# Sorted runs of 16 records instead of 8 in a four-layer graph network kernel

## The chip, the core and the metric

The kernel runs on one core of a Trainium2 chip. The metric is the device time of one execution in microseconds (us). The kernel before the change took 11441.29 us in the median of three runs (11425.31 to 11446.05).

## What is computed

Four graph layers over 12,500 nodes with 64 features and 212,500 directed edges (`src`, `dst`), sorted by `dst`. Each layer takes a layer norm and a relu of `x` and adds its result to `x`. Cut to the steps that matter here:

```python
h = relu(layernorm(x)); x = x + L0(h, edge_attr, src, dst)   # per-feature softmax over the edges of a dst
h = relu(layernorm(x)); x = x + L1(h, src, dst)              # mean of x[src] over the edges of a dst
h = relu(layernorm(x)); x = x + L2(h, src, dst)              # hyperbolic attention, summed by row = src
h = relu(layernorm(x)); x = x + L3(h, src, dst, edge_type)   # relational attention over the edges of a dst

# L2, the part that needs the edges in another order
u, v = -hh[row], hh[col]                  # row = src, col = dst
e = distance(u, v)                        # one number for each edge
attention = softmax of e over the edges with the same row
out[row] = sum of attention * log_h[col]
```

Layers 0, 1 and 3 sum over the edges of one `dst`, and the edges come sorted by `dst`. Layer 2 sums over the edges of one `src`, so the kernel sorts the edges by `src` itself, and only as far as it needs: into 98 blocks of 128 nodes.

## The kernel before

The program is a row of blocks, each with its own instruction streams for the engines, and a block ends when all its streams have ended: a preparation (to about 300 us), `softmax_edges(0)`, `finish_softmax`, `mean_edges`, `finish_mean`, `hyperbolic_edges`, `finish_hyperbolic`, `softmax_edges(3)`, `finish_relational`. The `*_edges` blocks are loops over edges in software-pipelined stages (`steps`, or `unrolled` in the mean loop): each engine runs its stage of several chunks in turn and waits on counters of the others. Four buffer slots (`SLOTS`) let the gathers run ahead.

The sort is spread over the first blocks. Partition p holds 1664 consecutive edges, cut into eight parts g of 208. A record is one float that packs `dst` and the node's place in its block of 128; an empty place holds 0.

- `softmax_edges(0)` counts the edges by block on the side.
- `finish_softmax` (L1512 to L1564) lays out where each group (part g, block b) goes. It pads every group to a multiple of `RUN` records, so that whole runs of `RUN` records can be moved. For each of the `PARTS * NK` pieces of 128 runs one DVE instruction (L1560) works out the runs' destinations, `dest`. POOL meanwhile issues 100 row gathers (L1339), and DVE waits for these afterwards (L1566).
- `mean_edges` sorts one part after another beside its own loop of 208 steps. POOL issues eight row gathers in each step (L922). PE turns the gathered rows (L934), DVE scans them (L1016), and in a turn of the sort DVE builds `hot_high` (L1047), 9 or 10 one-hot rows of `SORTED` columns, ACT builds `hot_low` (L986, L991), and PE multiplies both into `ps_sort` (L953), `SORTED` columns wide.
- `finish_mean` gathers 100 tiles of the mean (L1339), and behind them on the same POOL queue it scatters the sorted runs to `perm` in DRAM (`scatter_runs`, L1332): `PARTS * NK` indirect DMAs of 128 runs each. DVE computes the table of layer 2, and SP stores it with two DMAs (L1727, L1728). POOL waits at its end for the scatters, SP for the stores.
- `hyperbolic_edges` reads `perm` back as `NT` tiles of 128 records and runs `NT / 8` chunks (`CHB`) of eight tiles. A tile belongs to one block of `src`. For each tile POOL gathers 128 rows of `table2` by `dst` (L1148), SP loads the 128 rows of its block (L1134), DVE compares, PE turns the one-hot tile (L1179, moved by ACT at L1212), expands (L1188) and adds up (L1170), DVE carries the sum (L1321), and ACT stores it (L1224).

`NT` is fixed when the program is built, at the most that any graph could need: every group padded by `RUN - 1` and every block's last tile nearly empty, rounded up to 32 tiles. Tiles behind the last filled one are hollow: all their 128 records are 0, so that all 128 gathers of the tile read row 0 of `table2`; they go through the loop like the others.

```python
NK = -(-(P * PC + BLOCKS * (RUN - 1)) // (P * RUN))
SORTED = NK * RUN
NT = SLOTS * BT * -(-(E + PARTS * BLOCKS * (RUN - 1) + BLOCKS * (P - RUN)) // (P * SLOTS * BT))
```

Of the kernel before, what the change touches and what calls it, by code (L numbers as in the profile page):

```python
# [21 lines left out]
ALU = mybir.AluOpType  # L22
# [5 lines left out]
P = 128  # L28
# [17 lines left out]
ACC2 = D + 1  # L46
BLOCKS = -(-N // P)
BT = 8
RUN = 8
PARTS = 8  # L50
PC = PER // PARTS
NK = -(-(P * PC + BLOCKS * (RUN - 1)) // (P * RUN))
SORTED = NK * RUN
NT = SLOTS * BT * -(-(E + PARTS * BLOCKS * (RUN - 1) + BLOCKS * (P - RUN)) // (P * SLOTS * BT))
TRASH = NT * P // RUN
RUNS = TRASH + PARTS * NK * P
# [16 lines left out]
def build(nc, x, src, dst, edge_attr, edge_type, w0a, b0a, gamma, beta, w0b, b0b, scale0,  # L73
          w1, b1, w2, c2, w3, al3, ar3, b3, out):
    with ExitStack() as whole:
        def dram(name, shape, dt):
            return nc.dram_tensor(name, shape, dt, kind="Internal").ap()
# [3 lines left out]
        src3 = dram("src3", (EP,), I32)  # L81
        perm = dram("perm", (RUNS, RUN), F32)
        block_g = dram("block_g", (NT,), I32)
# [18 lines left out]
        def sb(name, shape, dt, ctx=whole):  # L102
            return ctx.enter_context(nc.sbuf_tensor(name, shape, dt))
# [56 lines left out]
        def stepper(eng, sem):  # L160

            count = [0]

            def step(ins):
                count[0] += 1
                ins.then_inc(sem, 1)
                eng.wait_ge(sem, count[0])
            return step
# [645 lines left out]
        def mean_edges():  # L814

            with nc.cleanup_on_exit(), ExitStack() as ctx:
                def buf(name, shape, dt=F32):
                    return sb(f"m_{name}", shape, dt, ctx)
# [18 lines left out]
                slot_i = buf("slot_i", [P, PC], I32)  # L837
                low_i = buf("low_i", [P, PC], I32)
                high_i = buf("high_i", [P, 2, PC], I32)
# [41 lines left out]
                with nc.Block() as block:  # L881
# [118 lines left out]
                    def _(dve):  # L1000
                        v = nc.vector
# [18 lines left out]
                        def divide(g):  # L1020

                            count = [0]

                            def step(ins):
                                count[0] += 1
                                ins.then_inc(split, 1)
                                dve.wait_ge(split, g * 5 + count[0])
                            dve.wait_ge(ranked, g * PC + PC)
                            step(v.tensor_copy(slot_i[:, :], slot_f[:, g, :]))
                            step(v.tensor_scalar(low_i[:, :], slot_i[:, :], 3, P - 1, ALU.logical_shift_right, ALU.bitwise_and))  # L1030
                            step(v.tensor_scalar(minus_low[:, g, :], low_i[:, :], -1.0, None, ALU.mult))
                            v.tensor_scalar(high_i[:, 0, :], slot_i[:, :], 10, 3, ALU.logical_shift_right, ALU.logical_shift_left)
                            step(v.tensor_scalar(high_i[:, 1, :], slot_i[:, :], RUN - 1, None, ALU.bitwise_and))
                            step(v.tensor_tensor(high_f[:, g, :], high_i[:, 0, :], high_i[:, 1, :], ALU.add))

                        def sort(p, w):
                            g = p - 1
                            if w == 0:
                                if g >= 0:
                                    divide(g)  # L1040
                                if p < PARTS:
                                    v.tensor_copy(ps_base[:, 0:BLOCKS], base[:, p, :]).then_inc(based, 1)
                                    dve.wait_ge(based, p + 1)
                            if g >= 0:
                                buffer_free(dve, g, w)
                                n0, n1 = cum(w), cum(w + 1)
                                v.tensor_tensor(hot_high[:, w % 2, 0:n1 - n0, :], ps_columns[:, None, 0:SORTED].broadcast_to([P, n1 - n0, SORTED]),  # L1047
                                                high_f[:, g, n0:n1][:, :, None].broadcast_to([P, n1 - n0, SORTED]),
                                                ALU.is_equal).then_inc(marked, 1)
                            if p < PARTS:  # L1050
                                for n in of_turn(w):
                                    at = p * PC + n
                                    if at >= 4:
                                        dve.wait_ge(ranked, at - 3)
                                    v.scalar_tensor_tensor(junk[:, at % 4, 0:BLOCKS + n], cat[:, p, 0:BLOCKS + n], cat[:, p, BLOCKS + n:BLOCKS + n + 1],  # L1055
                                                           ps_base[:, 0:BLOCKS + n], ALU.is_equal, ALU.mult,
                                                           accum_out=slot_f[:, p, n:n + 1]).then_inc(ranked, 1)
# [351 lines left out]
        def finish_softmax():  # L1409

            with nc.cleanup_on_exit(), ExitStack() as ctx:
# [26 lines left out]
                padded_i = sb("padded_i", [P, 2, HOT], I32, ctx)  # L1438
# [25 lines left out]
                with nc.Block() as block:  # L1464
# [34 lines left out]
                    def _(dve):  # L1499
                        v = nc.vector  # L1500
                        step = stepper(dve, ran)
# [5 lines left out]
                        def flat_b(a):  # L1507
                            return a[:, :, :].rearrange("p (t j) b -> p t (j b)", t=2)
# [1 line left out]
                        last = BLOCKS - 1  # L1510
                        dve.wait_ge(prefixed, 1)
                        step(v.tensor_scalar(padded_i[:, :, :], ps_y[:, :, 0:HOT], float(RUN - 1), None, ALU.add))  # L1512
                        step(v.tensor_scalar(padded_i[:, :, :], padded_i[:, :, :], 3, 3, ALU.logical_shift_right, ALU.logical_shift_left))
                        step(v.tensor_copy(flat_b(padded), padded_i[:, :, :]))
                        row = padded[:, :, :].rearrange("p g b -> p (g b)")
                        step(v.tensor_tensor_scan(out=upto[:, :, :].rearrange("p g b -> p (g b)"), data0=row, data1=row, initial=0.0,
# [508 lines left out]
```

## Time and profile before

| | |
|---|---|
| median of three runs | 11441.29 us |
| the profiled execution | 11452.29 us |
| its span, first to last instruction | 11450.6 us |
| its mean granted TensorE clock | 0.607 |
| PE, DVE, ACT, POOL busy | 59%, 62%, 35%, 67% |

The stages of the profiled execution by the timeline, in us from the span's start: `finish_softmax` 2453 to 2930, the mean loop to 5044, `finish_mean` 5058 to 5632, the hyperbolic loop 5653 to 8388. "Busy" is the time in which an engine carries out an instruction; waits, branches and issuing of a DMA by SP or ACT aren't counted. Idle time is put down to what ended it; "issue" means that the engine waited for nothing the profile shows. The DMA share is that of 16 DMA engines.

### The profile page before, as it was taken

What the parts mean: (1) busy time and instruction counts of PE and PEld (TensorE: products, weight loads), DVE (VectorE), ACT (ScalarE), POOL (GpSimd) and SP (SyncE); (2) the same over time, 40 slices, a digit from 0 to 9 for tenths busy, and PEclk for the clock granted to TensorE, in tenths of its full rate; (3) what the DMA queues carried; (4) which work ended last, traced back from release to release, by engine and by line L of the source; (5) the groups of instructions that cost most, each with busy time, mean ns of one, the idle gap of its engine ahead of it and who ended that gap; (6) DMA issues with size and microseconds to landing.
All of it is one profiled execution on the core that took longest, in us unless ns stands there. A gap on an engine that the chain in (4) does not pass through costs nothing. (4 is left out here: it accounts for less than half of the span.)

```text
span 11450.6 us, 134539 instructions
## 1 busy us (share of the span) xinstructions
PE 6752.2 (59%) x28079; PEld 5273.3 (46%) x28079; DVE 7082.5 (62%) x14431; ACT 4031.5 (35%) x8105; POOL 7668.6 (67%) x7662
## 2 busy tenths in 40 slices
PE   0777777733156666533277777777616677677660
PEld 0444444422045555533177777777613344444440
DVE  3666666663466666624466666666524588888882
ACT  0222222211057666731155555555410133333330
POOL 5777777761577777778666666666542577777774
PEclk9655566555578888865555555555555565555655
DMA  2444444440433333320344444444722344444441
GB/s 79 122 129 129 129 129 129 129 76 7 149 66 67 67 67 66 67 47 8 57 93 91 92 91 92 92 91 91 74 29 70 104 130 128 128 130 127 130 123 40
DMA packets 1419449, 1048.80 MB, mean 92 GB/s; under 512 B 921421, under 2 KB 1138032, under 8 KB 1418781
## 3 DMA queue, kind: packets, MB, share of 16 engines
q0 software_dynamic: 261824, 317.67, 17.5%
q1 hardware_dynamic: 762140, 367.42, 12.9%
q10 hardware_dynamic: 395317, 361.81, 9.8%
q8 instruction: 63, 1.03, 0.0%
q14 instruction: 105, 0.86, 0.0%
HBM read 576.48 MB, written 468.86 MB: 91 GB/s over the span
## 5 line engine op out<-in xcount | busy, mean ns | idle before, releaser
L1148 POOL DMA_INDIRECT h_rows_d<-table,h_idx_s x1824 | 1746.3, 957 | 976.3 <-issue 522.6
L609 POOL DMA_INDIRECT rows<-table3s,idx x1664 | 1648.2, 991 | 517.6 <-issue 501.5
L609 POOL DMA_INDIRECT rows<-table,idx x1664 | 1622.1, 975 | 550.0 <-issue 506.4
L922 POOL DMA_INDIRECT m_rows<-table,m_idx x1664 | 1571.5, 944 | 536.0 <-issue 500.6
L953 PE MATMUL m_ps_sort<-m_hot_high,m_hot_low 128*128 128x216 f32 x3328 | 920.4, 449 | 605.9 <-DVE m_hot_high L1047 532.8
L1188 PE MATMUL h_ps_src<-h_near,h_hot_t 128*128 128x65 f32 x3648 | 827.4, 418 | 722.8 <-DVE h_diff L1286 662.8
L1188 PEld LDWEIGHTS h_ps_src<-h_near,h_hot_t 128*128 128x128 f32 x3648 | 791.0, 329 | 807.5 <-issue 807.5
L953 PEld LDWEIGHTS m_ps_sort<-m_hot_high,m_hot_low 128*128 128x128 f32 x3328 | 825.2, 257 | 675.5 <-DVE m_hot_high L1047 567.1
L725 PE MATMUL ps_score<-ident,rows 128*128 128x128 f32 x1664 | 655.0, 497 | 572.4 <-DMA rows<-table,idx 568.0
L757 PE MATMUL ps_out<-ident,sums 128*128 128x128 f32 x3328 | 715.4, 384 | 286.5 <-DVE sums L680 286.5
L1170 PE MATMUL h_ps_sum<-h_rows_d,h_hot 128*128 128x65 f32 x3648 | 824.8, 417 | 13.2 <-DVE h_rows_d L1312 13.2
L757 PEld LDWEIGHTS ps_out<-ident,sums 128*128 128x128 f32 x3328 | 627.3, 222 | 423.6 <-DVE sums L680 280.2
L1170 PEld LDWEIGHTS h_ps_sum<-h_rows_d,h_hot 128*128 128x128 f32 x3648 | 805.3, 333 | 13.7 <-issue 13.7
L1321 DVE SCALAR_TENSOR_TENSOR h_run<-h_run,h_goes_on,h_ps_sum 128x65 f32<-128x65 f32 x1824 | 514.4, 282 | 468.9 <-PE h_ps_sum L1170 260.6
L1016 DVE TENSOR_TENSOR_SCAN m_sums<-m_same_b,m_sums,m_ps_rows 128x512 f32<-128x512 bf16 x208 | 266.2, 1280 | 868.7 <-issue 671.6
L725 PEld LDWEIGHTS ps_score<-ident,rows 128*128 128x128 f32 x1664 | 416.7, 311 | 831.4 <-issue 831.4
L785 ACT ACTIVATE ps_score<-ps_score 128x512 f32<-128x512 f32 x208 | 121.1, 582 | 1654.8 <-PE ps_score L727 1654.8
L774 ACT ACTIVATE wide<-rows 128x256 f32<-128x256 f32 x416 | 150.0, 407 | 1521.5 <-DMA rows<-table3s,idx 1521.5
L991 ACT ACTIVATE m_hot_low<-m_hot_low,record,m_slope 128x128 f32<-128x128 f32 x1664 | 660.0, 480 | 6.1
L628 DVE TENSOR_TENSOR hot<-bins,cat 128x784 bf16<-128x784 bf16 x208 | 202.9, 976 | 647.6 <-PE ps_count L713 647.6
L1055 DVE SCALAR_TENSOR_TENSOR m_junk<-cat,m_ps_base 128x98 f32<-128x98 f32 (+61 forms) x1664 | 586.9, 420 | 0.0
L727 PE MATMUL ps_score<-ident,attr 128*64 128x128 f32 x3328 | 578.3, 448 | 0.0
(420 smaller groups left out, 14858.5 us busy)
## 6 DMA issues: line engine op xcount, KB each, us to landing
scan<-out_e ACTq DMA_DIRECT2D x832, 256.0 KB
h_near<-table SPq DMA_DIRECT2D x1824, 32.5 KB
run_g<-h_run ACTq DMA_DIRECT2D x228, 260.0 KB
part_b<-part SPq DMA_DIRECT2D x832, 64.0 KB
max_b<-top ACTq DMA_DIRECT2D x416, 128.0 KB, 2.4
scan<-m_out_e SPq DMA_DIRECT2D x416, 128.0 KB
attr<-in_edge_attr SPq DMA_DIRECT2D x415, 128.0 KB
h_rows_d<-table,h_idx_s POOLq DMA_INDIRECT x1824
```

The costliest lines, as they stand in the source:

```text
L609: pool.indirect_dma_start(out=rows[:, b, k, h * GW:(h + 1) * GW], out_offset=None, in_=table3s.rearrange("n (q f) -> (n q) f", f=HEADS) if ...
L725: nc.tensor.matmul(ps_score[:, b % 2, k::TILES], rows[:, b, k, :], ident[:, :], start=True, stop=False)
L727: mm = nc.tensor.matmul(ps_score[h * D:(h + 1) * D, b % 2, k::TILES], attr[:, b, h, k, :], ident[:, :], start=False, stop=True)
L757: mm = nc.tensor.transpose(ps_out[:, j, k * P:(k + 1) * P], sums[:, b % 2, j, k::TILES], ident[:, :])
L922: pool.indirect_dma_start(out=rows[:, b, k, h * D:(h + 1) * D], out_offset=None, in_=table1, in_offset=bass.IndirectOffsetOnAxis(ap=idx[:, ...
L953: nc.tensor.matmul(ps_sort[:, 0:SORTED], hot_low[:, w % 2, j, :], hot_high[:, w % 2, j, :], start=n == 0, stop=n == PC - 1).then_inc(place ...
L991: ins = a.activation(hot_low[:, w % 2, j, :], hot_low[:, w % 2, j, :], ACT.Relu, bias=record[:, at:at + 1], scale=slope[:, at:at + 1])
L1055: v.scalar_tensor_tensor(junk[:, at % 4, 0:BLOCKS + n], cat[:, p, 0:BLOCKS + n], cat[:, p, BLOCKS + n:BLOCKS + n + 1], ps_base[:, 0:BLOCKS ...
L1148: pool.indirect_dma_start(out=rows_d[:, b, k, :], out_offset=None, in_=table2, in_offset=bass.IndirectOffsetOnAxis(ap=idx_s[:, b, k:k + 1] ...
L1170: mm = nc.tensor.matmul(ps_sum[:, k // HB, (k % HB) * ACC2:(k % HB + 1) * ACC2], hot[:, b, k, :], rows_d[:, b, k, D + 1:ROW2], start=True, ...
L1188: mm = nc.tensor.matmul(ps_src[:, k // HB, (k % HB) * (D + 1):(k % HB + 1) * (D + 1)], hot_t[:, b % 2, k * P:(k + 1) * P], near[:, b, k, : ...
L1321: v.scalar_tensor_tensor(run[:, b, k, :], before, goes_on[:, bass.ds(c * BT + k, 1)], ps_sum[:, k // HB, (k % HB) * ACC2:(k % HB + 1) * AC ...
```

## The change

`RUN` goes from 8 to 16, and the shifts that had 3 as log2 of 8 now take `RUN_BITS`. The sizes that follow from it by the formulas above: `NK` 27 to 14, so 112 destinations and scatters in place of 216; `SORTED` 216 to 224; `NT` 1824 to 1856 and `CHB` 228 to 232. A scatter moves 128 runs of 64 bytes in place of 32.

```diff
-RUN = 8
+RUN_BITS = 4
+RUN = 1 << RUN_BITS
...
-                            step(v.tensor_scalar(low_i[:, :], slot_i[:, :], 3, P - 1, ALU.logical_shift_right, ALU.bitwise_and))
+                            step(v.tensor_scalar(low_i[:, :], slot_i[:, :], RUN_BITS, P - 1, ALU.logical_shift_right, ALU.bitwise_and))
...
-                            v.tensor_scalar(high_i[:, 0, :], slot_i[:, :], 10, 3, ALU.logical_shift_right, ALU.logical_shift_left)
+                            v.tensor_scalar(high_i[:, 0, :], slot_i[:, :], 7 + RUN_BITS, RUN_BITS, ALU.logical_shift_right, ALU.logical_shift_left)
...
-                        step(v.tensor_scalar(padded_i[:, :, :], padded_i[:, :, :], 3, 3, ALU.logical_shift_right, ALU.logical_shift_left))
+                        step(v.tensor_scalar(padded_i[:, :, :], padded_i[:, :, :], RUN_BITS, RUN_BITS, ALU.logical_shift_right, ALU.logical_shift_left))
```

## Rows read from the trace of the kernel before

**Rows 1.** Page, costliest groups: busy us, mean ns, idle before, its releaser.

```profile
L1148 POOL DMA_INDIRECT h_rows_d<-table,h_idx_s x1824 | 1746.3, 957 | 976.3 <-issue 522.6
...
L922 POOL DMA_INDIRECT m_rows<-table,m_idx x1664 | 1571.5, 944 | 536.0 <-issue 500.6
```

**Rows 2.** Timeline, POOL and SP in finish_mean: start, us, instruction, idle before.

```profile
5520.12 0.98 SPq L1727 DMA_DIRECT2D table<-table_s  x1
5521.16 54.99 SPq L1728 DMA_DIRECT2D table<-G  x1
...
5594.77 0.97 POOL L1332 DMA_INDIRECT perm<-in_runs,dest  x1 [0.30 <-issue]
5634.28 0.23 POOL L1140 IOTA h_place<- 128x128 f32 x1 [38.55 <-POOLq L1703]
```

**Rows 3.** View of line L1332: ns min/median/max, first and last start.

```profile
L1332 POOL DMA_INDIRECT perm<-in_runs,dest x216: 965/970/9845, 5224.8 to 5594.8; - x108
```

**Rows 4.** DMA view by queue: packets, MB, share; 5560:5590, then 5600:5628.

```profile
q1 hardware_dynamic: 6686, 1.74, 42.6%
q0 software_dynamic: 741, 0.10, 3.3%
...
q1 hardware_dynamic: 6673, 1.71, 43.5%
q0 software_dynamic: 10, 0.00, 0.0%
```

**Rows 5.** Windows at finish_mean's end: last columns PEclk, DMA share, GB/s.

```profile
5626.00:5630.00 4.00, 0.00 (x0) 0.00 (x0) 0.00 (x0) 0.00 (x0) 0.00 (x0) 0.50 0.43 61
5630.00:5634.00 4.00, 0.00 (x0) 0.00 (x0) 0.00 (x0) 0.00 (x0) 0.00 (x0) 0.50 0.16 23
```

**Rows 6.** View of line L1560, and DVE's timeline behind it.

```profile
L1560 DVE SCALAR_TENSOR_TENSOR ut<-ut,run_no,n_ps_before x216: 306/314/318, 2494.3 to 2545.5; 128x99 f32<-128x99 f32 x108
...
2627.80 40.15 DVE L1566 RECIPROCAL big<-big 125x6400 f32<-125x6400 f32 x1 [81.56 <-DMA big<-scan,last_edge]
```

**Rows 7.** Mean loop: views of L1047 and L922, one turn's timeline.

```profile
L1047 DVE TENSOR_TENSOR m_hot_high<-m_ps_columns,m_high_f x184: 2155/2156/2382, 3205.3 to 5031.7; 128x1944 f32<-128x1944 f32 x176, 128x2160 f32<-128x2160 f32 x8
...
  issue: 500.6, 1643
  DMA m_idx<-src_g: 35.3, 21
...
3814.43 5.18 PE L953 MATMUL m_ps_sort<-m_hot_high,m_hot_low 128*128 128x216 f32 x18 [3.02 <-DVE m_hot_high L1047]
...
3820.25 0.65 PE L934 MATMUL m_ps_rows<-ident,m_rows 128*128 128x128 f32 x4 [0.64 <-DMA m_rows<-table,m_idx]
```

**Rows 8.** ACT's timeline, L1212: one instruction for each chunk.

```profile
7906.77 1.02 ACT L1212 ACTIVATE h_hot_t<-h_ps_hot 128x1024 f32<-128x1024 f32 x1 [3.68 <-PE h_ps_hot L1179]
...
8187.03 1.02 ACT L1212 ACTIVATE h_hot_t<-h_ps_hot 128x1024 f32<-128x1024 f32 x1 [3.65 <-PE h_ps_hot L1179]
...
8291.02 1.02 ACT L1212 ACTIVATE h_hot_t<-h_ps_hot 128x1024 f32<-128x1024 f32 x1 [5.50 <-PE h_ps_hot L1179]
...
8333.13 1.02 ACT L1212 ACTIVATE h_hot_t<-h_ps_hot 128x1024 f32<-128x1024 f32 x1 [29.47 <-PE h_ps_hot L1179]
```

**Rows 9.** Windows in the hyperbolic loop: PE, PEld, DVE, ACT, POOL, then DMA.

```profile
7000.00:7250.00 250.00, 188.94 (x866) 181.15 (x867) 161.03 (x514) 131.90 (x173) 165.11 (x173) 0.51 0.49 92
8155.00:8325.00 170.00, 79.55 (x364) 76.26 (x364) 70.55 (x229) 58.68 (x77) 76.30 (x80) 0.51 0.94 58
```

**Rows 10.** DVE's timeline at the two ends of the hollow stretch.

```profile
8153.87 0.17 DVE L1270 COPY h_idx_s<-h_idx_d 128x8 int32 x1 [0.49 <-issue]
...
8373.01 0.17 DVE L1284 TENSOR_TENSOR h_prod<-h_ps_src,h_rows_d 128x8 f32<-128x8 f32 x1 [4.78 <-DMA h_rows_d<-table,h_idx_s]
```

**Rows 11.** DMA view by queue, 7900:8070, then 8200:8370.

```profile
q0 software_dynamic: 3752, 7.83, 26.5%
...
q0 software_dynamic: 2376, 4.94, 74.8%
```

## The prediction

> **What bounds the kernel now.** I read the page first, then the timeline stage by stage, because no single engine bounds the whole: on the page POOL is busiest with 67%, and its largest groups are the row gathers [rows 1]. The question for each stage that the change touches is which stream ends last in it. There are four such stages.
>
> In `finish_mean` two streams end late. POOL issues the last of its 216 scatters at 5594.8 us and is idle for 38.55 us until the next block starts at 5634.3 [rows 2, 3]. SP issues the table's second store at 5521.2 [rows 2]; the hardware queue moves 1.71 MB in the 28 us from 5600 while the scatters' queue moves nothing [rows 4], and the DMA rate stays at 61 GB/s until 5630 [rows 5]. So the store ends this stage, not the scatters. The store waits for DVE's table, and DVE's table waits for the 100 gathers that stand ahead of the scatters on POOL: nothing on that chain is behind a scatter.
>
> In `finish_softmax` DVE is through with the destinations at 2546 and then waits 81.56 us for gathers [rows 6]. In the mean loop POOL issues without pause: 1643 of its 1664 gathers follow the one before at 0.30 us (500.6 us in all), and the other 21 lost 35.3 us [rows 7]. In the hyperbolic loop every engine has idle time; it is a cycle of waits with a fixed period, seen best in ACT's copy at L1212, which runs once in each chunk [rows 8].
>
> **The change part by part.** 1. *Scatters, 216 to 112.* By count 104 x 1.27 us (0.97 and 0.30 of issue) = 132 us leave POOL's queue [rows 3, 1]. None of it is on the path: the cover is the store, which starts at 5520.1 and lands at about 5632 whatever POOL does. The POOL queue has 97 us of stalls beside its 215 x 1.27 us; even if all of them stay, the 112th scatter goes out at 5224.8 + 111 x 1.27 + 97 = 5463, before the store begins. The price of a scatter of 64-byte runs isn't in the trace. Its lower bound is today's 0.97 us; the nearest row above it is the longest of today's, 9.85 us [rows 3]. It would have to average (5632 - 5225) / 112 = 3.6 us to become the end. I take 0.97, as a gather of 520-byte rows by the same engine takes 0.96 [rows 1]. What remains is contention: with scatters in flight the store's queue moves 1.74 MB in 30 us (58.0 GB/s), without them 1.71 in 28 (61.1) [rows 4]. From 5521 to 5596 that is 75 x 5% = 3.8 us, and the 60 scatters in it vanish. Term: -3.8, bounds 0 and -5.
>
> The Trainium skill (DMA: Bandwidth & Descriptors, Rules for kernel authors) advises to coalesce many small transfers, since below 64 KB one pays mostly overhead. By that rule halving the 4 KB scatters would bring their whole 132 us. The idle row behind the scatters says that it brings none of it.
>
> 2. *Destinations in `finish_softmax`, 216 to 112.* One follows the other every 0.238 us ((2545.5 - 2494.3) / 215), so DVE saves 24.8 us [rows 6]. It then waits 106 us in place of 81.56 for the gathers. Term 0.
>
> 3. *`SORTED` 216 to 224.* `hot_high` grows from 1944 to 2016 columns. Its two forms, 2156 and 2382 ns for 1944 and 2160, give 1.05 ns a column, so +0.08 us a turn. The 18 multiplications take 5.18 us and grow by 8/216, +0.19 us [rows 7]. They stand in one chain: turned rows, scan, `hot_high`, multiplications, next turned rows. PE idles 0.64 us there until the gathered rows land [rows 7], so +0.27 fits. If that cover were gone in all 184 turns, it would cost 50 us. Only the last turn, behind which no gather comes, shows: +0.3.
>
> 4. *Startup.* Two clears and DVE's unpacking grow by 1.8%; a few tenths. With the last term together +0.5.
>
> 5. *Four more chunks in the hyperbolic loop.* They aren't all of one kind. Counting the inputs' edges by part and block and padding each group as the kernel does gives 1729 filled tiles now and 1751 after, so 95 hollow ones become 105. The trace agrees: 1729 tiles end in chunk 216 of 228, and the DMA share rises from 0.49 to 0.94, with the rate falling from 92 to 58 GB/s, where chunk 216's gathers start at 8153.9 [rows 9, 10]. A gather of one and the same row costs the DMA engines more: 74.8% of 16 engines over 170 us for 2376 packets against 26.5% for 3752 [rows 11], 0.86 against 0.19 engine-us a packet.
>    - 22 filled tiles, 2.75 chunks. From 7906.77 to 8187.03 lie 24 chunks [rows 8], 11.68 us each: +32.1.
>    - 10 hollow tiles, 1.25 chunks. From 8155 to 8325 POOL issued 80 gathers, ten chunks, 17.0 us each at a DMA share of 0.94 [rows 9]. The lower bound is 11.68 (all hidden, +14.6). The whole hollow stretch, 8153.9 to the last chunk's rows at 8373.0 [rows 10], gives 219.1 / 11.875 = 18.5 (+23.1); the longest single spacing, 42.1 us [rows 8], gives +52.6. I take 17.0, as the stretch is bound by its DMAs: +21.3.
>
> Sum: -3.8 + 0.5 + 32.1 + 21.3 = +50.1 us, +0.44%. Against the profiled execution (11452.3, span 11450.6) that is 11502.4. The profiled one lies 11.0 us over the median of three, whose own spread is 21 us, so the forecast for the median is 11441.3 + 50.1 = 11491.4.
>
> **Rivals.** A. *The scatters set the end of `finish_mean`*, their last writes draining behind the store. Then the 38.55 us of idle time belong to them and move forward with them: the stage would end at 5463 + 38.6 = 5502 in place of 5634, -132, and the total would be 11441 - 132 + 54 = 11363, faster. It decides from the point at which the last scatter lands behind the store. This is the case in which the coalescing rule of the Trainium skill, named above, would show whole. Against it: SP's store alone starts at 5520, and only 10 packets of the scatters' queue are seen behind 5600 [rows 4]. 2%.
>
> B. *The hollow stretch's holes don't come back.* The longest spacing there holds a stall of 42.1 - 11.7 = 30 us [rows 8]. With another phase against the DMA queues it may vanish: 11461, no change that can be told. 5%.
>
> C. *One more such hole.* +30: 11521. The stretch gets 10% longer and depends on queueing, so it is likelier than B. 8%.
>
> D. *Empty places in the filled tiles.* Larger padding raises them from 8812 to 11628 (same count). Each reads row 0, too; at (0.86 - 0.19) x 32 / 128 = 0.17 engine-us for each of 2816, over 16 engines, it is 30 us if none is hidden: 11521. Against it the DMA share of 0.49 in the filled part [rows 9], where the chunks keep their period. 4%.
>
> E. *The mean loop becomes PE's.* If the 0.64 us aren't there in most turns, +50: 11541. PE can be late by several chunks before POOL's four slots are full, and POOL has not waited for it once [rows 7]. 2%.
>
> F. *The four chunks are absorbed.* It would need the loop's end to lie off the path; but the next block starts behind it. 1%.
>
> **How the numbers follow.** The forecast has 78%: 11491.4, its own range 11475 to 11508 (the hollow term's bounds -7 and +2, the store's 4, half of the runs' spread). With B on the one side and C and D on the other the range is 11461 to 11525. A measurement of this kernel can tell about 0.2% (23 us) from no change: faster means below 11418, slower above 11464. Faster: A, 2%. Same: B, F and the forecast's own tail, 8%. Slower: the rest, 90%.
>
> **What would show each step.** In the changed kernel's profile: scatters end by 5463, POOL's wait behind them grows to 170 us or more, the block still ends at about 5628 to 5631; L1560 has 112 instructions and DVE's wait behind it about 106 us; the mean loop ends within 1 us of today's; the period stays 11.68; the DMA share rises in chunk 218 or 219 of 232; the loop, 5653 to 8388 now, takes 53 us more. It would prove me wrong if the block after the scatters started 30 us earlier or more, if POOL waited for PE in the mean loop, if the period grew, or if the hollow stretch took less than 225 or more than 260 us.

## The result

The changed kernel takes 11471.9 us (11462.1 to 11487.6), the kernel before beside it 11439.4: ratio 1.0031, with an interval of 1.0018 to 1.0044, +32 us. Repeated later, it took 11479.1 against 11440.1: 1.0032 (1.0020 to 1.0044), +39 us. The sign is clear of noise in both. The change makes the kernel slower, inside the predicted range, and the time lies 12 to 20 us below the forecast of 11491.4.

The profiled execution took 11474.5 us, its span is 11471.7 and its granted clock 0.611. Its lines are one higher than those of before. First the page's two groups of gathers, then POOL and SP on the timeline at the end of `finish_mean`:

```profile
L1149 POOL DMA_INDIRECT h_rows_d<-table,h_idx_s x1856 | 1772.1, 955 | 996.4 <-issue 533.5
L923 POOL DMA_INDIRECT m_rows<-table,m_idx x1664 | 1570.8, 944 | 536.3 <-issue 499.8
```

```profile
5513.47 0.98 SPq L1728 DMA_DIRECT2D table<-table_s  x1
5514.51 50.93 SPq L1729 DMA_DIRECT2D table<-G  x1
5621.62 0.25 SPq L1119 DMA_DIRECT2D h_block_s<-block_g  x1
...
5419.84 0.97 POOL L1333 DMA_INDIRECT perm<-in_runs,dest  x1 [0.30 <-issue]
5621.65 0.23 POOL L1141 IOTA h_place<- 128x128 f32 x1 [200.85 <-POOLq L1704]
```

The view of the scatters' line (ns min/median/max, first and last start) and of the destinations' line:

```profile
L1333 POOL DMA_INDIRECT perm<-in_runs,dest x112: 965/969/9861, 5223.0 to 5419.8; - x112
...
L1561 DVE SCALAR_TENSOR_TENSOR ut<-ut,run_no,n_ps_before x112: 307/314/317, 2495.4 to 2521.9; 128x99 f32<-128x99 f32 x112
```

A scatter of 64-byte runs costs POOL what one of 32-byte runs did, 0.97 us [rows 3]. The 104 that are gone ended POOL's part 175 us earlier, and POOL then waits 200.9 us in place of 38.6 [rows 2]. The block still ended only 12.6 us earlier.

Last, ACT's copy that runs once a chunk, over 200 chunks (the 21st and the 221st) and across the longest spacing of the hollow stretch; then a window inside the hollow stretch:

```profile
5865.65 1.02 ACT L1213 ACTIVATE h_hot_t<-h_ps_hot 128x1024 f32<-128x1024 f32 x1 [4.40 <-PE h_ps_hot L1180]
...
8197.94 1.02 ACT L1213 ACTIVATE h_hot_t<-h_ps_hot 128x1024 f32<-128x1024 f32 x1 [4.39 <-PE h_ps_hot L1180]
...
8328.61 1.02 ACT L1213 ACTIVATE h_hot_t<-h_ps_hot 128x1024 f32<-128x1024 f32 x1 [5.50 <-PE h_ps_hot L1180]
8366.40 1.02 ACT L1213 ACTIVATE h_hot_t<-h_ps_hot 128x1024 f32<-128x1024 f32 x1 [25.99 <-PE h_ps_hot L1180]
```

```profile
8215.00:8405.00 190.00, 94.89 (x434) 91.03 (x435) 81.68 (x264) 67.85 (x89) 73.97 (x78) 0.51 0.87 60
```

200 chunks lie in 2332.3 us, 11.66 each, as before (11.68 over 24, [rows 8]). The hollow stretch shows the pattern of [rows 9]: two thirds of the filled part's instructions per us, a DMA share of 0.87, the rate down to 60 GB/s.

From one profile to the other, by first and last start: the mean loop's last gather 5036.8 to 5035.4 (-1.4), the next block after `finish_mean` 5634.2 to 5621.6 (-12.6), the first gather behind the hyperbolic loop (`acc_s`) 8395.4 to 8425.6 (+30.2). The loop with its drain took 42.9 us more. The rest of the difference (+21 at the end) lies in later blocks that the change doesn't touch, and it is scatter of the runs: from `acc_s` to the end it takes 3055.2 us before and 3046.2 here, but 3055.3 in the changed kernel's second profile.

### The profile page after: what moved, and what is told of

Same layout as the page of the kernel before. It is cut to its first block and busy times, and to the rows that moved or that the text cites. A ratio compares the mean times of both kernels' runs of the same rounds, so it can differ in the third digit from the quotient of the medians.

```text
span 11471.7 us, 135087 instructions
## 1 busy us (share of the span) xinstructions
PE 6778.1 (59%) x28239; PEld 5289.9 (46%) x28239; DVE 7102.6 (62%) x14319; ACT 4055.2 (35%) x8137; POOL 7550.0 (66%) x7590
## 5 line engine op out<-in xcount | busy, mean ns | idle before, releaser
L1149 POOL DMA_INDIRECT h_rows_d<-table,h_idx_s x1856 | 1772.1, 955 | 996.4 <-issue 533.5
L954 PE MATMUL m_ps_sort<-m_hot_high,m_hot_low 128*128 128x224 f32 x3328 | 939.6, 455 | 621.8 <-DVE m_hot_high L1048 548.2
```

Source lines behind the costliest of these rows:

```text
L954: nc.tensor.matmul(ps_sort[:, 0:SORTED], hot_low[:, w % 2, j, :], hot_high[:, w % 2, j, :], start=n == 0, stop=n == PC - 1).then_inc(place ...
L1149: pool.indirect_dma_start(out=rows_d[:, b, k, :], out_offset=None, in_=table2, in_offset=bass.IndirectOffsetOnAxis(ap=idx_s[:, b, k:k + 1] ...
```

## The experiments

The kernels ran in batches, each timed beside the kernel before on the same chip. **The first batch of four was on a chip on which the kernel before takes 14491 us; all others were on chips on which it takes 11440.** Both are told, the second kind first, since the forecast was made for it. Below, "the usual chip" and "the slower chip".

**1. What four hollow chunks cost.** The kernel before with more hollow tiles and nothing else.

```diff
-NT = SLOTS * BT * -(-(E + PARTS * BLOCKS * (RUN - 1) + BLOCKS * (P - RUN)) // (P * SLOTS * BT))
+NT = 1856
```

> The kernel before with 1856 tiles, that is four more chunks, all hollow, and nothing else (the kernel of e1_nt1856). On the chip of 11440 the marginal price of a hollow chunk decides the term that the forecast put at 17.0 us: 4 x 17.0 = +68 us (11508, ratio 1.0059) by the forecast's rate and by the long hollow stretch of the half-scatters run, whose 110 chunks came 17.4 us apart; +47 us (1.0041) if the holes are a fixed price of the stretch, as the pair of before and after (64 us of holes in both) suggests. As a hole comes every four to six chunks, four more chunks should bring about one hole of 25 us: 47 + 25 = 72. On the chip of 14491: +91 again.

Measured: 11503.8 us, ratio 1.0056 (1.0042 to 1.0071), +64 us, 16.0 us a chunk. By the interval that is 12.0 to 20.3, so the forecast's 17.0 holds and 11.68 is only just outside. The profiles say it more clearly: from the loop's first gather to the first of `acc_s` it takes 2804.9 us here, and 2733.3 to 2742.3 in three kernels with 1824 tiles, 17.0 us a chunk by their mean. ACT's copies in the hollow stretch show what the price is made of:

```profile
8360.13 1.02 ACT L1212 ACTIVATE h_hot_t<-h_ps_hot 128x1024 f32<-128x1024 f32 x1 [4.31 <-PE h_ps_hot L1179]
8372.25 1.02 ACT L1212 ACTIVATE h_hot_t<-h_ps_hot 128x1024 f32<-128x1024 f32 x1 [4.25 <-PE h_ps_hot L1179]
8389.52 1.02 ACT L1212 ACTIVATE h_hot_t<-h_ps_hot 128x1024 f32<-128x1024 f32 x1 [5.36 <-PE h_ps_hot L1179]
8414.36 1.02 ACT L1212 ACTIVATE h_hot_t<-h_ps_hot 128x1024 f32<-128x1024 f32 x1
```

About half of the spacings are 11 to 12.3 us, as in the filled part; others are 14 to 19, and then comes one of 25 to 43. Before has two of the long ones (27.7, 42.1), the changed kernel two (31.5, 37.8; in its second profile 32.0, 42.8), this one three (25.3, 36.9, 24.8). So the hollow stretch isn't slow evenly. Stretches at the period alternate with chunks that are late by 2 to 7 us, and every four to seven chunks a hole follows, which holds most of the loss (46 of 64 us in before).

**2. Half of the scatters.** Only the first 14 pieces of each part are scattered. This leaves part of the sort out: the records of the other 13 are missing, and empty ones stand in their places. POOL's wait at the block's end counts 14 a part, too.

```diff
-                for k in range(NK):
+                for k in range(14):
```

> The kernel before with only the first 14 of the 27 scatters of each part, 112 in all, each still of 32-byte runs. It leaves part of the sort out, so its output is not the reference's: part of the records are missing from the sorted list, and the hyperbolic loop finds empty records in their places, which all gather row 0. In finish_mean it isolates the count of scatters from their size: by the forecast's own term the store's contention alone goes, -4 us on the chip of 11440; on the chip of 14491, where the scatters are on the path, -137 us there. In the hyperbolic loop it is a test of rival D, that empty places cost DMA time: about half of the records turn empty. If an empty place costs 0.17 engine-us as the forecast worked out, some 100 thousand of them over 16 engines add up to 1000 us if none is hidden, and the period of 11.68 us must rise; if the period is kept, empty places in a filled tile cost nothing.

Measured: 12011.2 us, ratio 1.0504 (1.0490 to 1.0519), +571 us. In `finish_mean` it did what the change does: the store at 5516.1, the next block at 5624.3, 108.2 us behind it. As these are 112 scatters of 32-byte runs, the block is shorter because there are fewer, not because the runs are longer. In the loop it turned out to be no test of rival D. The missing records are the late ones of each part, so the first 118 chunks or so stayed as full as ever and the rest became hollow. The page's DMA row (tenths) shows the step:

```profile
DMA  2444444422322322202444488989871344444441
```

That makes it a long measurement of the hollow price. ACT's copies of the 118th and the last chunk:

```profile
6998.48 1.02 ACT L1212 ACTIVATE h_hot_t<-h_ps_hot 128x1024 f32<-128x1024 f32 x1 [3.58 <-PE h_ps_hot L1179]
...
8923.09 1.02 ACT L1212 ACTIVATE h_hot_t<-h_ps_hot 128x1024 f32<-128x1024 f32 x1 [4.82 <-PE h_ps_hot L1179]
```

110 chunks in 1924.6 us, 17.5 each, with 19 spacings over 24 us among them, one in 5.8 chunks. These 19 hold 397 of the 640 us above the period. The wanted part of the expectation, D in filled tiles, got no answer from this kernel.

**3. Empty records gather different rows.** An empty record's index becomes the number of its partition, with two small DVE instructions more in each half chunk.

```diff
+                            v.tensor_scalar(loc_i[:, 0:n], rec_i[:, 0:n], 0.0, lane[:, :], ALU.is_equal, ALU.mult).then_inc(u_step, 1)
...
+                            v.tensor_tensor(idx_d[:, at], idx_d[:, at], loc_i[:, 0:n], ALU.add).then_inc(u_step, 1)
```

> The kernel before, but an empty record gathers the row that has its own partition's number instead of row 0, two small DVE instructions more a half chunk. The kernel is that of e3_spread8, which ran on the chip of 14491 us; this asks for the chip of 11440. There the traces of both kernels show the price of the hollow stretch as a train of holes, one spacing of 28 to 43 us in every four to six chunks between spacings of 11.5 to 18, some 64 us above the period over about 12 chunks. Theory: the holes come from gathers of one and the same row, so with spread rows they go: the loop ends 60 us earlier, the total is 11380 (ratio 0.995), unless the two DVE instructions lengthen the filled chunks' period of 11.68. Rival: the holes belong to another thing that changes there (the empty tiles' slots, the stores of run_g), and stay: ratio 1.000. On the chip of 14491: same as before within 0.2%, as e3_spread8.

Measured: 11377.9 us, ratio 0.9948 (0.9934 to 0.9962), -62 us; 11380 was expected. The window of [rows 9] in this kernel:

```profile
8155.00:8325.00 170.00, 118.62 (x544) 113.65 (x543) 103.69 (x336) 84.10 (x112) 91.35 (x96) 0.52 0.38 77
```

The DMA share falls from 0.94 to 0.38 and all 228 chunks keep spacings of 6.5 to 13.5 us; no hole is left. So the holes belong to the gathers of row 0 by all 128 partitions; whether any other row read 128 times would do the same, no run asked. The filled part answers the question that experiment 2 left open: with the empty places of filled tiles spread, too, its 180 chunks from the 21st on take 11.66 us each, as before. They cost no time there. It is also the fastest version of the study.

**4. The changed kernel with spread rows and late scatters.** Beside the edit of experiment 3, POOL issues the scatters only when DVE has taken all of `lin1`.

```diff
+                        pool.wait_ge(lin1.taken, lin1.n)
                         scatter_runs(pool, scattered)
```

> The changed kernel with spread rows for empty records and with the scatters held back until DVE has taken lin1. On the chip of 11440: the changed kernel's +36, the wait's 0 (e8_late16) and the spread's -63, so -27 us, 11413 (ratio 0.9976): 4 chunks are then worth 4 x 11.68 = 47 us less 10 in finish_mean. Rival (the holes are not the same row's): +36, ratio 1.003. On the chip of 14491: e4_spread16 gave -88; if PE's signals crawl only because POOL issues scatters beside lin1, holding them back gives up to 100 us more, -190 (ratio 0.987); if lin2 crawls in its place, -88 again.

Measured: 11418.4 us, ratio 0.9982 (0.9973 to 0.9992), -21 us; 11413 was expected. Against experiment 3 the loop with its drain is longer by 46.7 us (2719.0 and 2672.3 us from the first gather to the first of `acc_s`), 4 x 11.68. With rows spread a hollow chunk costs what a filled one does. The start of the first gather of `acc_s`, the first of the two times in each line:

```profile
L1896 POOL DMA_INDIRECT acc_s<-run_g,final_row x100: 1205/1209/1223, 8325.5 to 8480.1; - x100
...
L1898 POOL DMA_INDIRECT acc_s<-run_g,final_row x100: 1205/1209/1226, 8372.1 to 8526.9; - x100
```

The first gather of the loop is at 5653.2 and 5653.1. In total this kernel is 40 us slower than that of experiment 3, so with the price of row 0 out of the way on both sides the change still costs its four chunks.

**5. Late scatters alone.** The changed kernel with the wait of experiment 4, and then the kernel before with it.

> The changed kernel, but POOL waits until DVE has taken all 25 groups of lin1 before it issues the first scatter. Theory: POOL's scatters delay PE's signals to ACT and DVE, on the chip where one lin1 group takes 33.6 us. There lin1 then needs some 50 us, its groups 1.25 to 2.41 us apart, and finish_mean gets shorter than in the changed kernel by up to the scatters' 147 us less those 50, so about -100 us against it, if the rest of DVE's chain, with its few hand-offs, is not slowed as much. On a chip where lin1 is not slowed: 112 scatters from about 5280 to 5480 instead of 5223 to 5420, still ahead of the store at 5514, so the same as the changed kernel within 5 us. Rival: the wait costs more than it gives, because lin2's groups now fall under the scatters and crawl in lin1's place: no gain on either chip.

Measured: 11476.7 us, ratio 1.0033 (1.0022 to 1.0044), +37 us, the same as the changed kernel. The scatters' view and SP's timeline:

```profile
L1333 POOL DMA_INDIRECT perm<-in_runs,dest x112: 965/969/9843, 5274.3 to 5497.2; - x112
...
5517.95 0.98 SPq L1728 DMA_DIRECT2D table<-table_s  x1
5518.98 50.93 SPq L1729 DMA_DIRECT2D table<-G  x1
5626.10 0.25 SPq L1119 DMA_DIRECT2D h_block_s<-block_g  x1
```

They end 21 us ahead of the store instead of 94, and the store takes the same 108.2 us to the next block.

> The kernel before, its 216 scatters held back until DVE has taken lin1. On the chip of 11440 it asks where the cover of the scatters ends: they would be issued from about 5275 to 5665 (370 to 390 us) instead of 5225 to 5595, the store lands near 5632. If the scatters then set the block's end, the next block starts 5 to 20 us behind the last one, at 5670 to 5685 instead of 5630, +40 to +55 us, ratio 1.0035 to 1.005; the point of rival A lies there, 35 us behind where the last scatter is issued today. If a scatter's landing doesn't count until much later, more. On the chip of 14491 it tests the crawl of lin1 under the scatters: if PE's signals are late only because POOL issues scatters, lin1 takes 50 us instead of 310, the later part of DVE's chain has few hand-offs, and it comes out up to 230 us faster than before (ratio 0.984); if the scatters slow lin2 or DVE's chain as much, 1.000.

Measured: 11455.8 us, ratio 1.0017 (1.0008 to 1.0026), +16 us. POOL in this kernel:

```profile
5644.18 0.97 POOL L1332 DMA_INDIRECT perm<-in_runs,dest  x1 [0.30 <-issue]
5655.85 0.23 POOL L1140 IOTA h_place<- 128x128 f32 x1 [10.70 <-POOLq L1703]
```

Here the scatters do set the end. The next block starts 10.7 us behind the end of the last one, at 5655.8, 22 to 26 us later than in the kernels with 216 scatters in their old place (5629.9 to 5634.2). I had expected 5670 to 5685. The 216 scatters took 364 us instead of up to 390, so that the last went out at 5644 and not at 5665; the time behind it is inside the 5 to 20 us expected. So the cover of the scatters before the change was about 25 us (an estimate from the next block's start at 5634.2, less the 11.6 us that lie here between the last scatter's start and the next block): the last could have gone out as late as about 5620 instead of 5595 without harm. It was real, but not wide.

**6. A wider sort.** The mean loop's one-hot matrix and multiplication 256 columns wide (`WIDE`) instead of 216, five times the change's step.

```diff
...
-                            mm = nc.tensor.matmul(ps_sort[:, 0:SORTED], ...
+                            mm = nc.tensor.matmul(ps_sort[:, 0:WIDE], ...
...
```

> The kernel before with the one-hot matrix of the mean loop and the multiplication by it 256 columns wide instead of 216 (the changed kernel has 224), five times the change's step. Nothing else differs and the output stays. The forecast's cover: PE idles 0.64 us a turn until the gathered rows land, and POOL never waits for PE. With 40 columns more, hot_high costs 0.42 us more a turn and the 18 multiplications 18 x 40/216 of 0.288 us, +0.96 us, so +1.4 us a turn. If PE's 0.64 us are all the cover there is, 184 turns give about +140 us; if DVE, PE and POOL have slack in different places and the loop is POOL's issue alone, 0 within 10 us. On the chip where POOL waits for its indices in this loop, 0 as well, unless PE's chain sets that wait.

Measured: 11515.2 us, ratio 1.0064 (1.0051 to 1.0078), +75 us, between the two answers. In the stretch from 3300 to 4800 us, POOL's gathers and PE's turned rows of before, of the changed kernel, and POOL's of this one:

```profile
L922 POOL DMA_INDIRECT m_rows<-table,m_idx x1202 | 1135.0, 944 | 366.3 <-issue 362.3 <-DMA m_idx<-src_g 4.0
L934 PE MATMUL m_ps_rows<-ident,m_rows 128*128 128x128 f32 x604 | 98.0, 286 | 96.6 <-DMA m_rows<-table,m_idx 96.3
...
L923 POOL DMA_INDIRECT m_rows<-table,m_idx x1202 | 1134.5, 944 | 366.3 <-issue 362.6 <-DMA m_idx<-src_g 3.7
L935 PE MATMUL m_ps_rows<-ident,m_rows 128*128 128x128 f32 x604 | 95.9, 281 | 69.5 <-DMA m_rows<-table,m_idx 69.4
```

```profile
L923 POOL DMA_INDIRECT m_rows<-table,m_idx x1161 | 1095.8, 944 | 406.1 <-issue 346.5 <-DMA m_idx<-src_g 59.6
```

PE's wait for the gathered rows is the cover. In 151 turns it is 96.3 us before and 69.4 after the change, 0.64 and 0.46 a turn, while POOL issues its 1202 gathers in either. With 256 columns it is 0, and POOL now waits 59.6 us in 145 turns, 0.41 a turn. The wait is named after an index load, but SP holds that load back until PE has turned the rows of four steps before (`slot_free(sp, turned, c, ago=SLOTS)`), and PE's turn starts some 22 us behind POOL's first gather of its step, where it was 11.2 behind before. Over the whole loop that is 60.9 us (2165.0 us from the first gather to the last, 2104.1 before), and another 12 us until the next block's first gather, as PE ends further behind POOL.

**7. The changed kernel again.**

> The changed kernel itself, unaltered. The four runs before this one were on a chip on which the kernel before takes 14491 us, not 11441; there, while POOL issued scatters, one group of lin1 took 33.6 us instead of 1.25 to 2.41, so finish_mean is bound by the scatters' count, and 104 fewer of them moved the table's first store up by 137 us. If this batch falls on such a chip: -146 (what runs of 16 with 1824 tiles measured) + 91 (what 1856 tiles measured) = -55 us, ratio 0.996, that is rival A of the prediction comes true there. If it falls on a chip on which the kernel before takes about 11440 us: the scatters are hidden, +32 us again (ratio 1.003), and the theory that the sign depends on whether hand-offs crawl under POOL's scatters stays possible. Rival (the slower chip only stretches everything alike): a ratio of 1.003 on either chip.

Measured on the usual chip, as given above: +39 us. Its store starts at 5516.9 and the next block 108.1 us later.

**8. On the slower chip.** The four kernels of the first batch, each against 14491 us.

> The kernel before with the tile count alone raised from 1824 to 1856: four more chunks, all of them hollow; scatters, padding and sort width as before. Prediction's price: 17.0 us for each hollow chunk, +68 us against the kernel before. Rival, read from the profile after: the hollow stretch loses some 64 us once, however long it is, and each further chunk costs the loop's period of 11.68 us, +47 us. A third, that the end of the loop is hidden, would give 0.

Measured: 14582.0 us, ratio 1.0052 (1.0031 to 1.0073), +91 us by the medians and +75 by the ratio (this is the kernel of experiment 1 on the other chip). A filled chunk takes longer here, too, 15.1 us in this profile in place of 11.66, and among its 15.9 hollow chunks stands one hole of 38.6.

> The changed kernel with the tile count held at 1824 (the inputs need 1751): runs of 16, 112 scatters and the wider sort remain, the four chunks are gone. Hollow chunks fall from 11.9 to 9.1. Prediction's prices: -3.8 (store) + 0.5 - 2.75 x (17.0 - 11.68) = -18 us against the kernel before. If a hollow chunk costs no more than a filled one, only finish_mean is left: -4 us by the prediction's contention term, -11 by the profile after. If the wider sort or the empty places in filled tiles cost anything, the result lies above that.

This is the changed kernel with the old 1824 tiles, whose last ones are hollow as before:

```diff
-NT = SLOTS * BT * -(-(E + PARTS * BLOCKS * (RUN - 1) + BLOCKS * (P - RUN)) // (P * SLOTS * BT))
+NT = 1824
```

Measured: 14345.0 us, ratio 0.9897 (0.9872 to 0.9922), -146 us. The expectation knew nothing of such a gain.

> The kernel before, with the index of every empty record changed from row 0 to the row of its own partition number (two more DVE instructions per half of the unpacking, one small iota), so that the gathers of a hollow tile read 128 different rows. If reading one and the same row is what makes the hollow stretch slow, its 64 us over the period go: -62 us, the DMA share stays near 0.5 to the end of the loop. If something else of the hollow stretch is slow (the one block loaded again and again, the stores), nothing changes but +2 us for the unpacking.

Measured: 14480.4 us, 1.0002 (0.9981 to 1.0023): no gain that can be told there from spread rows with runs of 8. In the kernel with runs of 16 and 1824 tiles, whose empty places all read row 0, the last 11 spacings of ACT's copies are 14.8 us on average against 15.2 in the filled part, so at this slower period its nine hollow chunks cost nothing above it.

> The changed kernel with the same change of the empty records' index. Then all four added chunks cost 11.68 us: against the spread kernel with runs of 8, +46.7 for the chunks and -4 to -11 for finish_mean, so +36 to +43. Against the kernel before: -62 + 40 = about -22. If the empty places in the filled tiles cost time by the one row (11628 of them here, 8812 before), this kernel would gain more from the spread than the one with runs of 8, by up to 29 us.

Measured: 14403.6 us, 0.9938 (0.9917 to 0.9959), -88 us. Against the kernel just above, from which it differs by the change alone, that is -77 us: 133 us won until the hyperbolic block starts, 60 lost in the loop (3517.1 and 3457.4 us from its first gather to the first of `acc_s`).

Where the -146 came from, SP's first store in the 1856-tile kernel of before (216 scatters) and in the one with runs of 16 (112), and behind each its scatters' view:

```profile
7132.00 0.98 SPq L1727 DMA_DIRECT2D table<-table_s  x1
...
L1332 POOL DMA_INDIRECT perm<-in_runs,dest x216: 968/972/6569, 6563.4 to 6846.2; - x108
```

```profile
6994.98 0.98 SPq L1728 DMA_DIRECT2D table<-table_s  x1
...
L1333 POOL DMA_INDIRECT perm<-in_runs,dest x112: 968/972/6602, 6561.1 to 6708.5; - x112
```

The scatters end 138 us earlier and the store starts 137 us earlier, in either kernel 286 us behind the last scatter. On the usual chip the store starts ahead of the last scatter [rows 2]. What waits is `lin1`, 25 groups of four transposes, a copy by ACT, four multiplications and an addition by DVE. The timeline of two groups in the kernel with 216 scatters, POOL left out:

```profile
6637.75 0.59 ACT L1393 ACTIVATE lin_rows_t<-lin_ps_t 128x500 f32<-128x500 f32 x1 [31.60 <-DMA m_idx<-src_g]
...
6638.39 1.94 PE L1384 MATMUL lin_ps_y<-w_t,lin_rows_t 128*125 128x64 f32 x8 [29.41 <-issue]
...
6640.12 1.04 PE L1369 MATMUL lin_ps_t<-ident,G 125*128 125x125 f32 x4
...
6660.15 0.42 DVE L1790 TENSOR_TENSOR X<-X,lin_ps_y 125x256 f32<-125x256 f32 x1 [33.18 <-DMA m_idx<-src_g]
6671.35 0.59 ACT L1393 ACTIVATE lin_rows_t<-lin_ps_t 128x500 f32<-128x500 f32 x1 [33.01 <-DMA m_idx<-src_g]
6671.99 1.94 PE L1384 MATMUL lin_ps_y<-w_t,lin_rows_t 128*125 128x64 f32 x8 [30.83 <-issue]
```

A group takes 33.6 us, with no engine longer at work than on the usual chip at the same granted clock of 0.50 (PE's multiplications 1.94 us against 1.78 to 1.94, ACT's copy 0.59 and DVE's addition 0.42 on both). PE's multiplications end at 6640.3 and DVE adds their result at 6660.15, 19.8 us later; PE's transposes end at 6641.2 and ACT copies them at 6671.35, 30.2 us later; ACT ends at 6671.94 and PE follows after 0.05 us. The first four groups, at the scatters' beginning, are still 2.4 to 5.0 us apart, and the crawl ends 15 to 25 us behind the last scatter; the rest goes at 2.4 and 1.25 us. (The releaser named, an index load of the block before, had long been done.) That what ACT and DVE do next starts 20 to 30 us behind PE's end while POOL issues scatters is what the lines show; whether PE's signal comes late or the engine that waits for it, they don't. Why it happens on that chip, and whether holding the scatters back behind `lin1` cures it, stays open: experiments 4 and 5 carried that question, but ran on the usual chip, where a group takes 1.25 to 2.41 us with scatters beside it. Nor did the changed kernel itself run on the slower chip. Three estimates from what did: -146 + 91 = -55 us (-71 with +75 in place of +91), the -88 of experiment 8's last kernel, which is the changed kernel with spread rows, and the -77 between the two kernels with spread rows. All say that there the change makes it faster.

## Why the prediction was right, and where its sizes were off

**The count of scatters is hidden.** Right on the usual chip. 104 fewer moved POOL's end by 175 us and the block's by 12.6. The last of the 112 goes out at 5419.8; the forecast's bound of 5463 kept all of today's 97 us of stalls, of which 56 were left. Late scatters confirm the cover from both sides: 112 that end 77 us later changed nothing (experiment 5), 216 that end 49 us later cost 16. Rival A was the right kind of rival with a decision point only 25 us away. The forecast worked that point out as 3.6 us a scatter, that is with all of 5225 to 5632 as room, and didn't say how little of it was left.

**The store's contention, -3.8.** The mis-sized term: it is -6.0 to -6.5. From the first store to the next block it takes 114.1 us before (114.3 to 114.6 in three experiments with 216 scatters in their old place) and 108.1 or 108.2 in the two profiles of the changed kernel and in experiments 2, 4 and 5 with 112. SP's own second issue accounts for 4.1 of it (54.99 to 50.93), the landing for the other 2. What costs is a scatter beside the store. The slower chip shows it, where all 216 go out ahead of the store (the kernel with 216 scatters and 1856 tiles):

```profile
7133.03 50.94 SPq L1728 DMA_DIRECT2D table<-G  x1
...
7240.17 0.25 SPq L1118 DMA_DIRECT2D h_block_s<-block_g  x1
```

There the store started at 7132.0, and it is 108.2 us again. The bound of -5 was too near, too. The next block starts at 5621.6, ahead of the 5628 to 5631 that the forecast named as a sign of the end; 2 us of that are this term's, the rest comes from the store's start, below. The loss was read from the rate in one 30 us window.

**The start of the store.** Between the profiles it moved from 5520.1 to 5513.5, which no term of the sum had. DVE's additions in `lin1` show where 4.6 us of it came from:

```profile
5242.51 0.42 DVE L1791 TENSOR_TENSOR X<-X,lin_ps_y 125x256 f32<-125x256 f32 x1 [1.99 <-PE lin_ps_y L1385]
5244.25 0.42 DVE L1791 TENSOR_TENSOR X<-X,lin_ps_y 125x256 f32<-125x256 f32 x1 [1.31 <-PE lin_ps_y L1385]
5245.51 0.42 DVE L1791 TENSOR_TENSOR X<-X,lin_ps_y 125x256 f32<-125x256 f32 x1 [0.83 <-PE lin_ps_y L1385]
```

Groups are 2.41 us apart while PE's granted clock is 0.50, its lower level of 1.2 GHz, and 1.25 once it is 1.00, the upper one of 2.4. PE is busy without a break ahead of the rise and behind it:

```profile
5234.00:5241.00 7.00, 7.00 (x36) 7.00 (x36) 1.26 (x3) 1.31 (x4) 5.48 (x6) 0.50 0.04 7
5246.00:5268.00 22.00, 22.00 (x212) 22.00 (x211) 7.16 (x17) 10.50 (x18) 16.66 (x18) 1.00 0.04 8
```

It rose behind the 4th group here and the 8th in before, but behind the 9th in the changed kernel's second profile, and between the 3rd and the 12th in the experiments. Of the other 2.0 us of the shift, 1.8 are the first group's earlier start. It is no effect of the change. With 216 scatters the store starts at 5515.5, 5516.7 and 5523.8 in experiments 1, 3 and 5, with 112 at 5516.1, 5516.9, 5518.0 and 5521.8 in experiments 2, 7, 5 and 4.

**Destinations, `SORTED`, startup: +0.5.** Right to 2 us: it came out at -1.4. L1561 has 112 instructions, DVE waits 104.3 us behind it where the forecast had 106, and the mean loop's first gather starts at 2931.7 instead of 2932.7. The mean loop's last gather moved by -1.4 and in the second profile by -1.4. Of rival E's cover 0.18 us a turn was used where the forecast had 0.27. With 0.64 there was room for a step three times as wide; experiment 6 shows the loop PE-bound at five times.

**Four more chunks, +53.4.** Right, and best seen over several profiles. From the loop's first gather to the first of `acc_s` it takes 2742.3 us before, 2735.6 in the late version of it and 2733.3 in experiment 6; 2785.1, 2790.3 and 2788.8 in the changed kernel, its repetition and its late version. The means differ by 51 us. The period of the filled part stayed at 11.66 us, with 2816 more empty places in it, so rival D is out: its 30 us over 219 chunks would be 0.14 each. Experiment 3 says the same from the other side. For the hollow chunks the forecast chose 17.0, between 11.68 and 18.5; experiment 1 gives 16.0 for four of them, experiment 2 17.5 over 110. For the 1.25 of the change the profiles leave 51 - 32.1 = 19 us, between the 14.6 of the plain period and the forecast's 21.3, and loops of one kind differ by 5 to 9 us among themselves. Rivals B and C took the hole of 30 us for an accident of one place that might go or be doubled. It isn't: it recurs in every four to seven chunks, which is why a rate read over ten chunks was a fair average price and a single spacing was not. But 1.25 chunks more need not meet a hole, and here they didn't. All three profiles of the changed kernel's loop have two holes, as those of before and of its late version do (in experiment 6 the first of two is split into two of 21 us), and ACT's copies there lie 62 to 67 us over the period, in the others 60 to 64. Only the four hollow chunks of experiment 1 bring a third hole, and 81 us.

**The sum.** With the measured sizes: -6.2 for the store, -1.4 for the mean loop, +51 for the hyperbolic loop, +43 in all, against +32 and +39 measured, whose intervals reach from +21 to +50. The start of the store and the blocks behind the loop add or take up to 9 us in single runs. That the forecast came out 12 to 20 us high is thus in part its hollow term and its small terms (2 us each) and the store (another 2), and for the rest the spread of the runs.

**The skill's rule.** The Trainium skill (DMA: Bandwidth & Descriptors, Rules for kernel authors) says to coalesce small transfers. On the usual chip its gain was 6 us of the 175 that POOL saved; on the slower one it was all of it, -137 us in the same block. The forecast tied the rule to rival A's mechanism, a late last write. What the traces of the slower chip show is another one, a chain of hand-offs that crawls beside the scatters, and that couldn't be seen in the trace of before.

## What to carry to other kernels

Fewer and larger indirect DMAs gain what the block's end was waiting for, not what the queue saves; work out how far the cover reaches, not only that it is there. When a size fixed for the worst case grows, ask what its padding does: here 47 of the loop's 51 us were chunks at its plain period, and the padding's own price, gathers that all read one row, could be had back, -62 us, by giving empty records different rows. A price that comes in bursts is read over several bursts and from several profiles, and a small addition may pay none of it.

## What the runs showed of the hardware that was not expected

A gather in which all 128 partitions read the same row (row 0 here) loads the DMA engines far more than one of different rows: the share is 0.94 and 0.38 in the same window, with 58 and 77 GB/s, though the same engine issues the same instructions in the same 0.95 us. Most of the cost doesn't come evenly, but as a hole of 25 to 43 us in every four to seven chunks. Where the loop's period is 15.2 us instead of 11.66, on the slower chip, nine hollow chunks cost nothing above it, and 15.9 had one hole.

A chip may run this kernel 27% slower with nearly the same instruction times. On the slower one a mean-loop gather takes 0.946 us and the 216 scatters even go out in 283 us instead of 370, but the waits are longer: POOL waits 726 us for indices in the mean loop, not 35, and 20 to 30 us pass from PE's end to the next start of ACT and DVE in `finish_mean`. By the three estimates above the sign of the change depends on it.
